# Attention seam and expert bias: joins, x with bias and part of the projection moved into the last unit, second bias as two rows

## The chip, the cores and the metric

One NeuronCore of a Trainium2 chip runs the kernel. The metric is the device time of one execution in microseconds (us), from runs of which the median is taken. TensorE (PE) multiplies, ScalarE (ACT), VectorE (DVE) and GpSimd (POOL) work element by element, SyncE (SP) issues nearly all DMAs. Each engine executes its instructions in order and is tied to the others by semaphores.

## What is computed

Three residual layers on x (8 x 64 tokens, 512 features), with a context of 8 x 1601 x 512:

```python
x = x + xattn(layernorm(x), ctx)      # 16 heads of 32 over 1601 keys: softmax(q k) v, then @ Wproj + bproj
x = x + attn(layernorm(x))            # 16 heads of 64, triu mask, only the diagonal of the softmax is used
x = x + moe(layernorm(x))             # 8 experts, each token goes to 2
# moe:  h = gelu(x @ W1[e] + b1[e]);  eo = h @ W2[e] + b2[e];  sum over e of gate[e] * eo
```

All is float32. Each operand of a large product is split in a high part (rounded to fp32r) and a low part (the rest), and a product is three matmuls: hi x hi, hi x lo, lo x hi.

## The kernel before

**Units.** Cross attention runs in 16 units, one for each batch element b and each of two chunks of the context (chunk 0: 7 tiles of 128 keys, chunk 1: 6). A unit has nine steps i = 0 to 8 over eight pairs of heads. In step i, TensorE turns the probabilities of pair i-1 (L816), computes scores for a later pair (L805), builds keys and values of the next chunk, and multiplies the turned probabilities with V (`outputs(i)`, L828). ScalarE casts the turned probabilities to PT (`probs_hi`, L505), and takes the exp of the next pair (L518). VectorE takes the maxima (L631), the low halves of PT (L640, L644) and the sum U of the two halves of the outputs (L676). PT has one buffer, so outputs(i), the turns of the next pair, `probs_hi` and the low halves form a loop. The last unit (BE, 1) has no keys and values left to make. Functions named `..._beside(i)` and `..._begin`, `..._between` put other work in its steps, on each engine at a fixed place.

**The seam.** The heads' outputs of batch elements 0 to 6 lie in DRAM (`o_heads`), each a sum over two chunks that must be weighted with factors. SP loads them as oA and the factors, spread over partitions, as oR (8 DMAs, L976). GpSimd adds the halves (L989), multiplies by oR (L1024) and joins the two chunks (L1027, `o_joined`). ScalarE and VectorE split the result in oT_hi (L1041) and oT_lo (L1104). Batch element 7 goes by another way: its U is moved by a product with sel7 (`new_outputs`, L1221), its factors are factor7 (four linked small operations on VectorE, L1130 to L1133), X7 (L1144) and a product with spread7 (L1252). `project` (L1210 to L1212) multiplies token tile t by Wproj, for contraction blocks m. VectorE adds the products to x_sum (`first_sum`, L1158), which holds x + bproj (L1162). `norm_vector` and `norm_scalar` normalise the sum, first for tiles 0 to 2, then for tile 3; TensorE turns it (L1265, L1271), ScalarE and VectorE split it in x2T_hi and x2T_lo (L1189, L1192), and the next layer's Q columns begin (L155). W2_hi and W2_lo are the parts of that layer's weights (L943 on ScalarE, L1018 and L1291 on GpSimd). `keep_busy` (L166) issues matmuls whose result is not used.

**The experts.** Weights come as 8 units of 1 MB for each expert through a ring of four (L1684), cast by ScalarE (L1851) and split by VectorE (L2034). Tokens are sorted by expert in DRAM into tiles of 128, ten in this run. For a tile TensorE makes hidden layer and output; the bias b1 enters as a product of ones with two rows, high and low part, in a tile of 128 partitions whose other rows are zero (L2146). b2 was loaded for each expert over all 128 partitions (L1696) and added by VectorE to the output (L2061).

SP's order around the change: old outputs, chunk factors out (L963), head weights 0 (L937), oR, bvc, Wp_raw, x_sum, bproj, head weights 1. GpSimd's order: halves, masks, W2_lo, joins.

## Time and profile before

| | us |
|---|---|
| median of 3 runs | 1383.21 (1383.02 to 1383.8) |
| the profiled execution | 1381.99 |
| its span, first to last instruction | 1380.2 |
| TensorE busy | 1335.9 (97%) |
| VectorE busy | 932.7 (68%) |
| ScalarE busy | 763.7 (55%) |
| GpSimd busy | 107.5 (8%) |
| mean granted TensorE clock | 0.997 of full |

A row of the timeline gives start and length in us, the engine, the line of the kernel, the operation and its tiles (output <- inputs), the count, and in brackets the idle time of the engine before it and what ended that. A row with a count above one merges neighbours, and its length runs to the end of the last. The chain is the work that ended last, followed back from the end: time on it is time of the kernel. The windows give each engine's busy time in a stretch.

### The profile page before, as it was taken

What the parts mean: (1) busy time and instruction counts of PE and PEld (TensorE: products, weight loads), DVE (VectorE), ACT (ScalarE), POOL (GpSimd) and SP (SyncE); (2) the same over time, 40 slices, a digit from 0 to 9 for tenths busy, and PEclk for the clock granted to TensorE, in tenths of its full rate; (3) what the DMA queues carried; (4) which work ended last, traced back from release to release, by engine and by line L of the source; (5) the groups of instructions that cost most, each with busy time, mean ns of one, the idle gap of its engine ahead of it and who ended that gap; (6) DMA issues with size and microseconds to landing.
All of it is one profiled execution on the core that took longest, in us unless ns stands there. A gap on an engine that the chain in (4) does not pass through costs nothing.

```text
span 1380.2 us, 22335 instructions
## 1 busy us (share of the span) xinstructions
PE 1335.9 (97%) x7573; PEld 1163.0 (84%) x7574; DVE 932.7 (68%) x1506; ACT 763.7 (55%) x1334; POOL 107.5 (8%) x85
## 2 busy tenths in 40 slices
PE   9999999999999999999999999988899989999998
PEld 7898988898889898888988989977688778888886
DVE  5566666667567666666666766658588956388885
ACT  6465555566456555555555655555331636478872
POOL 2000000000000000000000000035444130000002
PEclk9999999999999999999999999999999999999999
DMA  5211111110201112101111111274527566399993
GB/s 198 96 54 32 30 45 52 27 46 24 56 15 53 30 34 61 30 27 46 46 34 33 36 30 34 48 137 116 92 62 288 209 227 200 129 350 346 354 368 113
DMA packets 126854, 145.13 MB, mean 105 GB/s; under 512 B 64073, under 2 KB 67529, under 8 KB 126801
## 3 DMA queue, kind: packets, MB, share of 16 engines
q1 hardware_dynamic: 125536, 140.44, 32.9%
q0 software_dynamic: 1280, 4.20, 0.9%
q8 instruction: 23, 0.38, 0.1%
q14 instruction: 15, 0.11, 0.0%
HBM read 124.75 MB, written 19.86 MB: 105 GB/s over the span
## 4 chain that ended last, share of the span: by engine, by line
PE 77%; DVE 12%; issue 5%; ACT 3%; DMA 2%; SPq 1%; DVEq 0%; POOL 0%; ACTq 0%
PE ps_scores L155 13%; PE ps_scores L157 13%; PE ps_scores L156 13%; PE ps_out L828 6%; PE ps_turn L816 5%; PE ps_scores L805 5%; PE ps_out L2172 2%; PE ps_out L2174 2%; PE ps_out L2173 2%; PE ps_turn L706 2%; PE ps_scores L2151 2%; PE ps_scores L2149 2%; PE ps_scores L2150 2%; DVE stat L631 2%; DVE Ks L556 1%
## 5 line engine op out<-in xcount | busy, mean ns | idle before, releaser
L556 DVE SCALAR_TENSOR_TENSOR Ks<-ps_scores,bkc,Ks 64x384 fp32r<-64x384 f32 (+2 forms) x254 | 160.5, 632 | 143.3 <-ACT Ks L430 140.8
L155 PE MATMUL ps_scores<-cT_hi,Wkv_hi 128*128 128x384 f32 (+2 forms) x504 | 182.0, 361 | 0.0
L518 ACT ACTIVATE Pr<-ps_scores,stat 128x705 f32<-128x705 f32 (+1 forms) x128 | 119.5, 934 | 109.9 <-DVE stat L631 109.9
L157 PE MATMUL ps_scores<-cT_hi,Wkv_lo 128*128 128x384 f32 (+2 forms) x504 | 173.0, 343 | 0.0
L156 PE MATMUL ps_scores<-cT_lo,Wkv_hi 128*128 128x384 f32 (+2 forms) x504 | 172.5, 342 | 0.0
L562 DVE TENSOR_TENSOR Vs<-ps_scores,Vs 128x512 fp32r<-128x512 f32 (+1 forms) x103 | 71.2, 691 | 147.9 <-ACT Vs L434 147.2
L430 ACT ACTIVATE Ks<-ps_scores,bkc 64x384 fp32r<-64x384 f32 (+2 forms) x254 | 149.4, 588 | 39.1 <-PE ps_scores L157 35.5
L155 PE MATMUL ps_scores<-Wkv_hi,cT_hi 128*128 128x512 f32 (+1 forms) x412 | 170.0, 413 | 0.0
L505 ACT CAST PT<-ps_turn 128x512 fp32r<-128x512 f32 (+2 forms) x256 | 110.2, 483 | 102.1 <-PE ps_turn L816 101.3
L157 PE MATMUL ps_scores<-Wkv_hi,cT_lo 128*128 128x512 f32 (+1 forms) x412 | 161.8, 393 | 0.0
L156 PE MATMUL ps_scores<-Wkv_lo,cT_hi 128*128 128x512 f32 (+1 forms) x412 | 161.1, 391 | 0.0
L2034 DVE TENSOR_TENSOR wu_lo<-wu_raw,wu_hi 128x2048 fp32r<-128x2048 f32 x56 | 126.7, 2287 | 21.1 <-ACT wu_hi L1851 21.1
L640 DVE TENSOR_TENSOR PT<-ps_turn,PT 128x512 fp32r<-128x512 f32 (+2 forms) x256 | 130.0, 549 | 11.0 <-ACT PT L505 10.0
L828 PE MATMUL ps_out<-PT,Vs 128*128 128x256 f32 x832 | 123.1, 286 | 13.9 <-DVE PT L644 9.6
L434 ACT CAST Vs<-ps_scores 128x512 fp32r<-128x512 f32 (+1 forms) x103 | 60.4, 586 | 133.8 <-PE ps_scores L157 133.0
L828 PEld LDWEIGHTS ps_out<-PT,Vs 128*128 128x128 f32 x832 | 113.3, 189 | 24.6 <-DVE PT L644 12.7
L631 DVE TENSOR_REDUCE stat<-ps_scores 128x1 f32<-128x705 f32 (+1 forms) x128 | 125.7, 983 | 3.5 <-DVE stats L682 3.4
L816 PE MATMUL ps_turn<-ident,Pr 128*128 128x128 f32 x832 | 112.2, 273 | 0.0
L1851 ACT CAST wu_hi<-wu_raw 128x2048 fp32r<-128x2048 f32 x56 | 105.3, 1917 | 4.9 <-DMA wu_raw<-in_L_ffn_W_dram 4.6
L816 PEld LDWEIGHTS ps_turn<-ident,Pr 128*128 128x128 f32 x832 | 98.2, 141 | 5.7
L157 PEld LDWEIGHTS ps_scores<-cT_hi,Wkv_lo 128*128 128x128 f32 x504 | 94.8, 188 | 5.2
L156 PEld LDWEIGHTS ps_scores<-cT_lo,Wkv_hi 128*128 128x128 f32 x504 | 95.2, 189 | 4.0
(391 smaller groups left out, 2500.0 us busy)
## 6 DMA issues: line engine op xcount, KB each, us to landing
wu_raw<-in_L_ffn_W_dram SPq DMA_DIRECT2D x64, 1024.0 KB, 7.2
raw<-in_ctx_dram SPq DMA_DIRECT2D x16, 768.0 KB, 4.6
raw<-in_ctx_dram SPq DMA_DIRECT2D x8, 1024.0 KB, 5.2
raw<-in_ctx_dram SPq DMA_DIRECT2D x8, 512.0 KB
sorted_x<-zeros SPq DMA_DIRECT2D x1, 4096.0 KB, 15.3
sorted_out<-zeros SPq DMA_DIRECT2D x1, 4096.0 KB, 25.6
o_heads<-U SPq DMA_DIRECT2D x56, 64.0 KB, 1.7
oA<-o_heads SPq DMA_DIRECT2D x8, 448.0 KB, 9.1
```

Source lines behind the costliest of these rows:

```text
L155: nc.tensor.matmul(out_ap, sh, mh, start=(i == 0), stop=False)
L156: nc.tensor.matmul(out_ap, sh, ml, start=False, stop=False)
L157: last = nc.tensor.matmul(out_ap, sl, mh, start=False, stop=(i == len(pairs) - 1))
L430: ins = nc.scalar.activation(Ks[c][0:64, 2 * i + h, o:o + wide], acc[64 * h:64 * h + 64, 0:wide], ACT.Identity, bias=bkc[:, 2 * i + h:2 * ...
L505: ins = nc.scalar.copy(PT[:, full[0]:full[-1] + 1, 0, :], acc[:, 0:P * len(full)].rearrange("p (t r) -> p t r", r=P))
L518: nc.scalar.activation(Pr[:, i % 2, 0:VALID[c]], S_cols(c, 0, VALID[c], 0 if ctx else i % 2), ACT.Exp, bias=stat[:, 0, c, i:i + 1], accum_ ...
L556: ins = nc.vector.scalar_tensor_tensor(out=Ks[c][64:128, j, o:o + wide], in0=acc[64 * h:64 * h + 64, 0:wide], scalar=bkc[:, j:j + 1], in1= ...
L631: nc.vector.tensor_reduce(stat[:, 0, c, i:i + 1], S_cols(c, 0, VALID[c], 0 if ctx else i % 2), AX.X, ALU.max, negate=True).then_inc(sem("s ...
L640: ins = nc.vector.tensor_tensor(PT[:, full[0]:full[-1] + 1, 1, :], acc[:, 0:P * len(full)].rearrange("p (t r) -> p t r", r=P), f32(PT[:, f ...
L816: ins = nc.tensor.matmul(bank(P_BANKS[q])[0:M, at:at + P], Pr[:, (i - 1) % 2, t * P:t * P + M], ident[:, :], is_transpose=True, start=True ...
L828: ins = nc.tensor.matmul(psO_heads, Vs[c][0:M, t, i - 1, :], PT[0:M, t, :, :].rearrange("p a r -> p (a r)"), start=(t == 0), stop=(t == CH ...
L2034: nc.vector.tensor_tensor(wu_lo[v][:, :, :], wu_raw[v % RING][:, :, :], f32(wu_hi[v][:, :, :]), ALU.subtract).then_inc(sem("wu_lo_done"), 1)
```

## The change

In the last unit and the seam: oR is loaded as soon as the last chunk-0 scores are made, then Wproj and bproj, before the head weights; x_sum comes after Wp_lo, whose raw input shares its place. The joins stand ahead of three of the masks and of W2_lo on GpSimd, which also adds bproj to x. Wp_hi is cast by ScalarE at the end of the unit before, Wp_lo follows in step 0, oT_hi in steps 2 to 5, oT_lo in steps 3 to 6, W2_hi[0] in two halves in steps 6 and 7. Token tile 0 and a block of tile 1 are projected inside the unit, with fewer `keep_busy`. The second layer's normalised x is written by ScalarE for tiles 0 to 2, with a shift, as the third layer's is. In the experts: b2 is split in high and low part with b1, written to DRAM, loaded as two rows for each expert, and added by a product of ones in TensorE's last part of the output; VectorE copies where it added. Some tiles move in SBUF.

```diff
-            sp.wait_ge(sem("kv_made"), KV_LAST + PIECES[1])
-            load_head_weights(sp, 0)
-            sp.wait_ge(sem("o_summed"), PAIRS_0 + NP + 1)
+            sp.wait_ge(sem("s_made"), PAIRS_0 + NP)
             sp.wait_ge(sem("r_out"), 32)
             for c in range(2):
                 for jj in range(2):
                         r0 = 64 * jj + HD * h
                         src = r_dram[c, h].rearrange("(m jj) t -> jj m t", jj=2)[jj][:, 0:OLD]
                         sp.dma_start(oR[r0:r0 + HD, c, :, :], src.partition_broadcast(HD)).then_inc(sem("oR_in"), 16)
+            sp.dma_start(Wp_raw[:, :, :], Wproj.rearrange("(k p) n -> p k n", p=P)).then_inc(sem("wp_in"), 16)
+            sp.wait_ge(sem("oA_in0"), 64)
+            sp.dma_start(bpr[:, :], bproj.partition_broadcast(P)).then_inc(sem("x_again"), 16)
+            sp.wait_ge(sem("kv_made"), KV_LAST + PIECES[1])
             sp.dma_start(bvc[:, :], bkv[D:2 * D].rearrange("(m p) -> p m", p=P),
                          allow_slow_non_contiguous=True).then_inc(sem("bv_in"), 16)
-            sp.dma_start(Wp_raw[:, :, :], Wproj.rearrange("(k p) n -> p k n", p=P)).then_inc(sem("wp_in"), 16)
+            load_head_weights(sp, 0)
+            sp.wait_ge(sem("wp_lo"), 1)
             sp.dma_start(x_sum[:, :, :], x_rows).then_inc(sem("x_again"), 16)
-            sp.wait_ge(sem("oA_in0"), 64)
-            sp.dma_start(bpr[:, :], bproj.partition_broadcast(P)).then_inc(sem("x_again"), 16)
             load_head_weights(sp, 1)
...
+            pool.wait_ge(sem("o_added"), 2 * KC)
+            pool.wait_ge(sem("oR_in"), 128)
+            for m in range(KC):
+                join(m)
+            nc.gpsimd.memset(triu[:, :, :], 1.0).then_inc(sem("masks_set"), 1)
+            nc.gpsimd.memset(diag[:, :], 0.0).then_inc(sem("masks_set"), 1)
+            nc.gpsimd.memset(spread7[:, :, :], 0.0).then_inc(sem("masks_set"), 1)
+            pool.wait_ge(sem("masks_set"), 4)
...
+            pool.wait_ge(sem("x_again"), 32)
+            for t in range(TT):
+                ins = nc.gpsimd.tensor_tensor(x_sum[:, t, :], x_sum[:, t, :], bpr[:, :], ALU.add)
+            ins.then_inc(sem("x_base"), 1)
             pool.wait_ge(sem("sw_hi"), 1)
-            nc.gpsimd.tensor_tensor(W2_lo[0][:, :, :], W2_raw[0][:, :, :], f32(W2_hi[0][:, :, :]), ALU.subtract) \
-                .then_inc(sem("sw_lo"), 1)
-            pool.wait_ge(sem("oR_in"), 128)
-            for m in range(KC):
-                pool.wait_ge(sem("o_added"), KC + m + 1)
-                for c in range(2):
-                    nc.gpsimd.tensor_tensor(oA[c][:, 0, m, :], oA[c][:, 0, m, :], oR[:, c, m, :], ALU.mult) \
-                        .then_inc(sem("o_scaled"), 1)
-                pool.wait_ge(sem("o_scaled"), 2 * m + 2)
-                nc.gpsimd.tensor_tensor(oA[0][:, 0, m, :], oA[0][:, 0, m, :], oA[1][:, 0, m, :], ALU.add) \
-                    .then_inc(sem("o_joined"), 1)
+            for k in range(KC):
+                ins = nc.gpsimd.tensor_tensor(W2_lo[0][:, k, :], W2_raw[0][:, k, :], f32(W2_hi[0][:, k, :]), ALU.subtract)
+            ins.then_inc(sem("sw_lo"), 1)
...
+            elif i == 8:
+                act.wait_ge(sem("wp_in"), 16)
+                act.wait_ge(sem("o_made"), PAIRS_0 + NP)
+                nc.scalar.copy(Wp_hi[:, :, :], Wp_raw[:, :, :]).then_inc(sem("wp_hi"), 1)
 
         def scalar_old_hi(act, m):
             act.wait_ge(sem("bv_in"), 16)
             if i == 0:
                 act.wait_ge(sem("o7_turned"), 1)
                 nc.scalar.copy(o7[:, 0, 0, :, :], o7_bank(0)).then_inc(sem("o7_in"), 1)
-            elif i == 1:
-                head_weights_hi(act, 0)
-            elif 4 <= i < NP:
-                if i == 5:
-                    act.wait_ge(sem("wp_in"), 16)
-                    nc.scalar.copy(Wp_hi[:, :, :], Wp_raw[:, :, :]).then_inc(sem("wp_hi"), 1)
-                elif i == 7:
-                    act.wait_ge(sem("shifted7"), 1)
-                    nc.scalar.activation(part7[:, :, :], part7[:, :, :], ACT.Exp).then_inc(sem("exp7"), 1)
-                scalar_old_hi(act, i - 4)
+            elif 2 <= i < 2 + KC:
+                scalar_old_hi(act, i - 2)
+            elif i == 6:
+                act.wait_ge(sem("sw_in0"), 64)
+                nc.scalar.copy(W2_hi[0][:, 0:2, :], W2_raw[0][:, 0:2, :])
+            elif i == 7:
+                act.wait_ge(sem("shifted7"), 1)
+                nc.scalar.activation(part7[:, :, :], part7[:, :, :], ACT.Exp).then_inc(sem("exp7"), 1)
+                nc.scalar.copy(W2_hi[0][:, 2:KC, :], W2_raw[0][:, 2:KC, :]).then_inc(sem("sw_hi"), 1)
...
+            act.wait_ge(sem("ln_scaled"), 2)
+            for t in FIRST_TILES:
+                ins = nc.scalar.activation(xn2[:, t, :], x_sum[:, t, :], ACT.Identity,
+                                           bias=shift2[:, t:t + 1], scale=lnt2[4][:, t:t + 1])
+            ins.then_inc(sem("x_base"), 1)
+            norm_scalar(act, 3, lnt2, LAST_TILE)
             turned_hi(0)
             turned_hi(1)
-            norm_scalar(act, 3, lnt2, LAST_TILE)
...
-            if i == 5:
-                vector_old_lo(dve, 0)
-            elif i == 6:
+            if i == 0:
+                dve.wait_ge(sem("wp_hi"), 1)
+                nc.vector.tensor_tensor(Wp_lo[:, :, :], Wp_raw[:, :, :], f32(Wp_hi[:, :, :]), ALU.subtract) \
+                    .then_inc(sem("wp_lo"), 1)
+            elif 3 <= i < 3 + KC:
+                vector_old_lo(dve, i - 3)
...
-                dve.wait_ge(sem("wp_hi"), 1)
-                nc.vector.tensor_tensor(Wp_lo[:, :, :], Wp_raw[:, :, :], f32(Wp_hi[:, :, :]), ALU.subtract) \
-                    .then_inc(sem("wp_lo"), 1)
-            elif i == 7:
-                vector_old_lo(dve, 1)
...
-            dve.wait_ge(sem("x_again"), 32)
-            nc.vector.tensor_tensor(x_sum[:, :, :], x_sum[:, :, :],
-                                    bpr[:, :].unsqueeze(1).broadcast_to([P, TT, D]), ALU.add) \
-                .then_inc(sem("x_base"), 1)
-            vector_old_lo(dve, 2)
-            vector_old_lo(dve, 3)
...
-            norm_vector(dve, 2, x_sum, xn2, lnt2, FIRST_TILES, prepare=summed)
+            norm_vector(dve, 2, x_sum, xn2, lnt2, FIRST_TILES, prepare=summed, shift=shift2)
...
-            elif i in (2, 3):
+            elif i == 5:
                 pe.wait_ge(sem("o7_in"), 1)
-                keep_busy(3, 6)
-            elif 4 <= i < 7:
-                keep_busy(1, 6)
+                pe.wait_ge(sem("wp_lo"), 1)
+                project(pe, 0, (0,))
+            elif i == 6:
+                project(pe, 0, (1,))
             elif i == 7:
-                keep_busy(1, 6)
                 pe.wait_ge(sem("o_summed"), PAIRS_1 + NP - 1)
                 new_outputs(pe, 1, slice(0, KC - 1))
-                keep_busy(6, 6)
             elif i == 8:
-                pe.wait_ge(sem("o7_in"), 1)
-                pe.wait_ge(sem("wp_lo"), 1)
-                for t in FIRST_TILES:
-                    project(pe, t, (0,))
+                project(pe, 0, (2, 3))
+                project(pe, 1, (0,))
...
-            for t in FIRST_TILES:
-                project(pe, t, range(1, KC))
+            project(pe, 1, range(1, KC))
+            project(pe, 2, range(KC))
...
-            pe.wait_ge(sem("ln_done"), 2)
+            pe.wait_ge(sem("x_base"), 2)
...
-            keep_busy(8, SPREAD_BANK)
-            pe.wait_ge(sem("ln_done"), 3)
+            keep_busy(3, SPREAD_BANK)
+            pe.wait_ge(sem("ln_done"), 2)
...
-                sp.dma_start(b2row[:, :], b2[bass.ds(e, 1), :].rearrange("a d -> (a d)").partition_broadcast(P)) \
-                    .then_inc(sem("b2row_in"), 16)
+                sp.dma_start(f32(b2rows[0:2, :]), b2_dram[:, bass.ds(e * D, D)]).then_inc(sem("b2row_in"), 16)
...
-            sp.dma_start(b1_raw[:, :], b1.rearrange("e (c p) -> (e c) p", p=P)).then_inc(sem("b1_in"), 16)
+            sp.dma_start(b_raw[:, 0:P], b1.rearrange("e (c p) -> (e c) p", p=P)).then_inc(sem("b1_in"), 16)
+            sp.dma_start(b_raw[:, P:P + B2], b2.rearrange("e (c p) -> (e c) p", p=B2)).then_inc(sem("b1_in"), 16)
...
+            for part, half in enumerate((b_hi, b_lo)):
+                sp.dma_start(b1_dram[part].rearrange("(r c) -> r c", c=P), f32(half[:, 0:P])) \
+                    .then_inc(sem("b1_out"), 16)
+                sp.dma_start(b2_dram[part].rearrange("(r c) -> r c", c=B2), f32(half[:, P:P + B2])) \
                     .then_inc(sem("b1_out"), 16)
             load_next(0, 5)
-            sp.wait_ge(sem("b1_out"), 32)
+            sp.wait_ge(sem("b1_out"), 64)
...
+            pool.wait_ge(sem("x_sorted"), 16 * 2 * TT)
+            pool.wait_ge(sem("g_turned"), 1)
+            nc.gpsimd.memset(f32(b2rows[:, :]), 0.0).then_inc(sem("b1rows_zeroed"), 1)
...
-                dve.wait_ge(sem("b2row_in"), 16 * (e + 1))
                 dve.wait_ge(sem("eo_stored"), t * 16 + EO_CREDIT)
-                nc.vector.tensor_tensor(eo[:, :], bank(7), b2row[:, :], ALU.add) \
+                nc.vector.tensor_copy(eo[:, :], bank(7)) \
...
+                    if q == QT - 1:
+                        pe.wait_ge(sem("b2row_in"), 16 * (e + 1))
+                        nc.tensor.matmul(bank(7), ones_r[:, :], b2rows[:, :], start=False, stop=False)
```

## Rows read from the trace of the kernel before

**Rows 1.** The page, section 4: the chain that ended last, by engine.
```profile
PE 77%; DVE 12%; issue 5%; ACT 3%; DMA 2%; SPq 1%; DVEq 0%; POOL 0%; ACTq 0%
```

**Rows 2.** Waits of ScalarE, 905 to 985 us: total us, times, longest.
```profile
ACT oT_hi L1041 <- POOL oA L1027: 4.8, 3, 3.0
```

**Rows 3.** Timeline of SP: start and length of issue, line, target, count.
```profile
903.79 1.26 SPq L963 DMA_DIRECT2D chunk_factors<-factorT  x2
...
919.77 2.95 SPq L937 DMA_DIRECT2D sW_raw<-in_L_attn_WQ_dram  x4
922.81 5.51 SPq L976 DMA_DIRECT2D oR<-chunk_factors  x8
```

**Rows 4.** Landing (us after issue), rate in 40 slices of 919 to 950, chain.
```profile
chunk_factors<-factorT SPq DMA_DIRECT2D x2, 32.0 KB, 5.7
...
GB/s 0 0 63 243 274 223 215 233 238 217 189 204 227 194 220 215 194 222 213 167 174 354 367 396 381 388 383 386 319 252 228 77 227 193 228 37 0 21 0 0
...
927.89 9.10 DMA oR<-chunk_factors
```

**Rows 5.** Timeline of the last unit (start, us): ScalarE exp and Wp_hi, TensorE.
```profile
922.24 0.85 ACT L518 ACTIVATE Pr<-ps_scores,stat 128x705 f32<-128x705 f32 x1 [1.88 <-DVE stat L631]
922.57 1.96 PE L1221 MATMUL ps_turn<-U,sel 128*128 128x256 f32 x8 [0.46 <-issue]
926.81 0.95 PE L828 MATMUL ps_out<-PT,Vs 128*128 128x256 f32 x6 [0.98 <-issue]
...
932.26 1.43 PE L828 MATMUL ps_out<-PT,Vs 128*128 128x256 f32 x6 [2.53 <-DVE PT L644]
...
936.54 0.96 PE L828 MATMUL ps_out<-PT,Vs 128*128 128x256 f32 x6
...
939.73 0.99 PE L828 MATMUL ps_out<-PT,Vs 128*128 128x256 f32 x6 [0.71 <-DVE PT L644]
...
942.82 1.91 ACT L1053 CAST Wp_hi<-Wp_raw 128x2048 fp32r<-128x2048 f32 x1
...
946.94 0.98 PE L828 MATMUL ps_out<-PT,Vs 128*128 128x256 f32 x6 [1.48 <-DVE PT L644]
...
957.18 0.98 PE L828 MATMUL ps_out<-PT,Vs 128*128 128x256 f32 x6 [0.23 <-DVE PT L644]
```

**Rows 6.** Timeline of VectorE and GpSimd where both read SBUF.
```profile
930.75 4.53 POOL L1018 TENSOR_TENSOR sW_lo<-sW_raw,sW_hi 128x2048 fp32r<-128x2048 f32 x1 [6.94 <-ACT sW_hi L943]
...
948.30 0.58 DVE L1113 TENSOR_TENSOR top<-stat 128x8 f32<-128x8 f32 x1
...
948.92 1.07 DVE L1116 TENSOR_TENSOR part<-top,stat 128x16 f32<-128x16 f32 x1
...
949.91 2.28 DVE L1119 TENSOR_TENSOR Wp_lo<-Wp_raw,Wp_hi 128x2048 fp32r<-128x2048 f32 x1
```

**Rows 7.** Windows: busy us of each engine (PE first), PEclk, DMA share, GB/s.
```profile
932.00:936.00 4.00, 3.74 (x17) 3.74 (x18) 2.23 (x6) 1.67 (x6) 3.28 (x1) 0.57 1.10 224
...
978.00:982.00 4.00, 2.20 (x8) 1.69 (x8) 4.00 (x6) 2.76 (x3) 0.95 (x1) 0.79 0.94 146
```

**Rows 8.** Timeline of the seam: the third sum, the link, first Q matmul.
```profile
967.28 0.69 DVE L1158 TENSOR_TENSOR x_sum<-x_sum,ps_scores 128x512 f32<-128x512 f32 x1 [0.18 <-PE ps_scores L1212]
...
974.18 2.43 DVE L132 TENSOR_TENSOR rs<-rt 128x1 f32<-128x1 f32 x1
...
980.27 0.77 PE L155 MATMUL ps_turn<-x2T_hi,sW_hi 128*128 128x512 f32 x1 [1.80 <-DVE x2T_lo L1192]
```

**Rows 9.** Timeline of the same chain in front of the experts.
```profile
1090.54 0.69 DVE L1895 TENSOR_TENSOR x_sum<-x_sum,ps_scores 128x512 f32<-128x512 f32 x1 [0.69 <-PE ps_scores L1539]
...
1099.62 0.68 DVE L1922 TENSOR_TENSOR x3T_lo<-ps_scores,x3T_hi 128x512 fp32r<-128x512 f32 x1
```

**Rows 10.** Experts, lines view (busy us, mean ns); a window as in rows 7.
```profile
L2146 PE MATMUL ps_scores<-b1rows,ones_r 128*128 128x512 f32 x36 | 15.0, 416 | 0.0
...
1240.00:1300.00 60.00, 59.11 (x275) 47.94 (x274) 50.90 (x34) 49.12 (x42) 0.00 (x0) 1.00 1.00 349
```

66 lines of the change are left out of this document (37 added, 29 removed).

## Prediction, made before the change was run

> **What bounds the kernel now.** The page's chain comes first: TensorE carries 77% of it [rows 1], so a stall counts only where it stops TensorE or ends last. The change touches four stretches: the last attention unit (920 to 958 us), the seam behind it (to 980 us), the start of the experts (1080 to 1126 us) and the expert loop (to 1370 us).
>
> In the last unit the waits show ScalarE held 4.8 us by GpSimd's joins of the old heads' outputs [rows 2]. The joins start late because their factors oR were issued at 922.81 us, behind the head weights, and landed at 936.99 us (927.89 + 9.10) [rows 3, 4]. The reader is to see the rhythm of the `outputs` matmuls in [rows 5]: the natural step is 3.19 us (936.54 to 939.73), but outputs 1 to 6 took 20.13 us instead of 16.0, and 6 to 8 took 10.24 us. In the seam, the first Q matmul waits for VectorE: from the third `first_sum` (967.28) to 980.27 us are 12.99 us, of which one 128x1 operation took 2.43 us [rows 8]. The experts' loop is TensorE's: even where transfers are at share 1.00 it is busy 59.11 of 60 us [rows 10].
>
> **Part 1, loads.** oR now waits only for unit 7's last chunk-0 scores (about 909 us) and r_out. r_out's first store starts at 903.79 [rows 3] and the pair needs 5.7 us to land [rows 4]; the second started 0.65 us after the first, so oR starts at 910.2 us. Of the eight, 229,376 bytes each, 1.84 MB at the about 210 GB/s that such rows move [rows 4] take 8.75 us. The first bytes move 1.3 us after an issue (sW_raw issued 919.77 [rows 3], rate row up at about 921), and a landing shows 2.0 us after the last byte (2.88 MB of weights and oR from 921.3 would end at 935.0, the landing is at 936.99). So oR lands at 910.2 + 1.3 + 8.75 + 2.0 = 922.3 us, 14.7 us earlier. Wp_raw, 1.05 MB at 385 GB/s [rows 4], follows 2.7 us later: 925.0 us. The weights of head unit 0, now behind both, are wanted at step 6 only; x_sum waits for Wp_lo and lands at about 936 us, before GpSimd asks for it.
>
> **Part 2, the start of the last unit: a new wait.** ScalarE's cast Wp_hi (1.91 us [rows 5]) stands before the exp of pair 0, and waits for Wp_raw. Queued behind it is that exp, which began at 922.24 us [rows 5], and behind the exp TensorE's turns, so all of the unit. The exp now starts at 925.0 + 1.9 = 926.9. From exp to outputs 1 were 4.57 us (922.24 to 926.81), of which 0.9 was TensorE finishing the new outputs (922.57 + 1.96 = 924.53 [rows 5]) after the exp was ready; so 926.9 + 3.7 = 930.6. VectorE's Wp_lo (2.28 us) now stands before the low halves of pair 1 and can meet a GpSimd join; I add 0.4 of a possible 1.1. Outputs 1: **931.0 us, 4.2 later** than 926.81.
>
> **Part 3, the rest of the unit.** The joins run from 922.3 to about 938 us (3 operations of 1.14 us each, four times, plus up to 2.28 for Wp_lo), each done before its ScalarE step; the joins' waits are gone. W2_hi leaves step 1 and goes in halves (0.96 us) into steps 6 and 7, where the 3.19 us step has 1.1 us of ScalarE free. The two projections in steps 5 and 6, 3 matmuls of 0.23 us each, fit under TensorE's wait. Steps 1 to 6 would take 5 x 3.19 = 16.0 us. Two costs come on top. The clock: before, step 2 to 3 took 4.28 us while the granted clock fell to 0.57 [rows 5, 7], 1.1 us over natural. Now TensorE idles longer, from 923.6 to 928 us, and the filler matmuls are gone; I take the same 1.1. And oT_lo, which reads two SBUF tiles, meets GpSimd's new x additions: up to one of them (about 1.1 us) at each meeting, as `top` and `part` in [rows 6]; with oT_lo VectorE's step is nearly full, so this shows: 0.7 in all, bounds 0 and 2.2. Outputs 6: 931.0 + 17.8 = 948.8 us (before 946.94).
>
> Steps 6 to 8 took 10.24 us. Wp_lo (2.28) and one oT_lo (0.68) leave VectorE's path: 7.3. But GpSimd's W2_lo moves from step 2 to behind ScalarE's cast in step 7: 4 operations of about 1.2 us (a quarter of 4.53 [rows 6], and the start of each), running from 0.6 to 5.5 us after outputs 7. VectorE starts factor7 1.45 us after outputs 7; three of its four links read two SBUF tiles. [rows 6] show such links of 128x8 and 128x16 elements taking 0.58 and 1.07 us instead of about 0.17: each waits for the GpSimd operation that runs, the next one then slips in. So each of the three ends with a GpSimd operation, at 2.0, 3.4 and 4.8 us, instead of the last at 2.25: +2.5 us. Outputs 8: 948.8 + 7.3 + 2.5 = **958.6 us, 1.4 later** than 957.18.
>
> The Trainium skill, SBUF — State Buffer, Who interferes with whom, says that a VectorE instruction with two SBUF inputs contends with a GpSimd instruction that reads SBUF, and, under SBUF: two separate sides, that the one that starts first has the pair for the whole instruction. The trace [rows 6] agrees with the lock. By the rule alone VectorE may also win the gaps and lose one operation only: the sum would be lower by 1.5 to 2.5 us, rival B below.
>
> **Part 4, the seam.** Off VectorE go x + bias (2.28) and two oT_lo (1.27), but behind them it waited for the copy of o7 in any case, so only some 0.8 us of start is won. TensorE's projection shrinks by 6 matmuls, and the third sum, no longer held by it, starts 9.1 us after outputs 8 instead of 10.1 (957.18 to 967.28): 1.0 won. From there the new order is one the kernel already has in front of the experts: third sum 1090.54, last low half at 1099.62 + 0.68 = 1100.30: 9.76 us [rows 9], against 12.99. That includes ScalarE's three normalisations (2.22 us for VectorE's 1.46), and it does without the 2.43 us link, which stood behind a GpSimd operation that is now released only after the last tile. 3.2 won. Together **-4.2 us**. Nothing new is late: the K weights' low part is done some 9 us before use.
>
> The clock at the first Q matmuls is 0.79 over 978 to 982 us already [rows 7]; TensorE now idles 3.4 us before the turns where it idled 1.2, with 3 fillers for 8. Turns at the lower level would cost 0.4; I take **+0.4** (bounds -1.6, the eight slow matmuls gone, and +1.5).
>
> **Part 5, experts.** One more matmul for each of 10 tiles: like the b1 product, 36 of these lie at 0.236 us spacing on TensorE (0.416 in their overlapped record [rows 10]). In the last tile it hides under VectorE's fetched sums; 9 x 0.236 = 2.1 us. Each b2 load falls from 256 KB to 4 KB, 0.7 us of transfer at 349 GB/s. Where that can be felt, 1240 to 1300 us, TensorE lacks 0.9 us in all [rows 10]; I take 0.6 back. **+1.5 us** (bounds 0 and +2.2). The wait for the row moves from VectorE to TensorE, behind which the next tile queues; the row is issued with the previous tile's result and wanted 20 us later, with a longest landing of 8.0 us for the larger form. At the start SP issues three more small DMAs (b2 in, two parts out, some 0.4 us each), which delay unit 5's weights by about 1 us against 10 us of slack; the wider casts add 0.1 us under up's matmuls; the memset of b2rows delays its load by 0.6 us with 4 to spare: 0. The copy that replaces the add in the last tile is worth -0.1 to 0.
>
> **Sum**: 1.4 - 4.2 + 0.4 + 1.5 = -0.9 us. The profiled execution took 1381.99 us around its span of 1380.2; the median of the runs is 1383.21. The difference is applied to the median: **1382.3 us**. About 2.8 us (0.2%) is what a measurement of this kernel tells from no change.
>
> **The rivals.**
> A, the forecast: gain in the seam, given back by Wp_hi's wait, by the lock in step 7 and by the matmuls. 0.50; own range 1380.5 to 1385.5.
> B, no collision in step 7: W2_lo loses the gaps to VectorE, or starts late enough. -2.5 more: 1379.8 us. For it: the rows show only two links in a row, and the lock could go to VectorE between GpSimd's operations. Against: both of these lost that gap. 0.25, and mostly beyond the 0.2%.
> C, slower: without fillers the clock stays low through the unit. Each of the five steps then costs 1.1 us as step 2 to 3 did, +4.4 more: 1386.7 us. It decides from the first step on at which TensorE's work no longer lifts the clock; for it: that idle of 4.4 us; against: in the low level TensorE was busy 3.74 of 4 us and the clock rose again [rows 7]. The Trainium skill, TensorE: Matmul & The Clock Gate, What's actually happening, has the throttled state as the default that activity releases, which speaks against fewer fillers. 0.13.
> D, the b2 product is free: TensorE's matmul fills the loop's waits and the lighter loads give back the rest, -1.5: 1380.8 us; with an earlier Wp_raw (by 1 us) 1379.8. 0.12.
>
> **How the numbers follow.** Faster takes 0.22 of B, 0.06 of A and 0.06 of D: 0.34. Slower takes the 0.12 of C and 0.04 of A: 0.16. The rest, 0.50, is within 0.2%. The range takes A's and D's and most of B and goes up to near C: 1379.0 to 1386.2.
>
> **What would show it.** Right: oR landed by 923 us; a ScalarE gap before Wp_hi ending near 925; outputs 1 near 931; links of factor7 of about 1 us; seam of about 19 us from outputs 8 to Q; tiles longer by 0.24 us. Wrong: Wp_raw there by 922 (3 us better), factor7 links of 0.2 us, a granted clock below 1.00 beyond 936 us, or a TensorE wait for b2rows.

## The result, and the profile after

The changed kernel takes **1379.18 us** (median of 17 runs, 1377.41 to 1382.37) beside 1383.21 us of the kernel before in the same session: ratio 0.9974, 95% interval 0.9967 to 0.9981, so 3.6 us faster by the ratio, between 2.6 and 4.6. The profiled execution took 1380.16 us around a span of 1377.4; it lies 1.0 above its median, and that of the kernel before 1.2 below its own, so the two traces show less of the gain than the medians do.

The page after: span, engines' busy time, and the chain that ended last.

```profile
span 1377.4 us, 22276 instructions
PE 1333.5 (97%) x7541; PEld 1158.8 (84%) x7542; DVE 930.1 (68%) x1503; ACT 766.4 (56%) x1338; POOL 114.1 (8%) x93
...
PE 80%; DVE 11%; issue 4%; ACT 3%; DMA 2%; SPq 0%; DVEq 0%; ACTq 0%
```

TensorE's share of the chain rose from 77% [rows 1] to 80%: waits went away, its work did not. Where they went is read from six marks, each the start of the same instruction in both traces:

| mark, us | before | after | difference |
|---|---|---|---|
| outputs 1 of the last unit | 926.81 | 929.70 | +2.9 |
| outputs 8 | 957.18 | 956.31 | -0.9 |
| third sum of the seam | 967.28 | 966.97 | -0.3 |
| first Q matmul | 980.27 | 978.22 | -2.1 |
| third sum ahead of the experts | 1090.54 | 1086.95 | -3.6 |
| last `eo` | 1372.02 | 1369.01 | -3.0 |

The loads and the start of the last unit (timelines of SP, GpSimd, ScalarE and TensorE; start, length, engine, line).

```profile
910.38 3.64 SPq L975 DMA_DIRECT2D oR<-chunk_factors  x8
914.06 0.43 SPq L976 DMA_DIRECT2D Wp_raw<-in_L_xattn_Wproj_dram  x1
...
921.93 2.22 POOL L995 TENSOR_TENSOR oA<-oA,oR 128x448 f32<-128x448 f32 x2
...
924.00 1.90 ACT L1050 CAST Wp_hi<-Wp_raw 128x2048 fp32r<-128x2048 f32 x1 [3.79 <-DMA Wp_raw<-in_L_xattn_Wproj_dram]
925.81 0.84 ACT L519 ACTIVATE Pr<-ps_scores,stat 128x705 f32<-128x705 f32 x1
...
929.70 1.62 PE L829 MATMUL ps_out<-PT,Vs 128*128 128x256 f32 x6 [1.38 <-issue]
```

oR is issued 12.4 us earlier than in [rows 3], and the joins run. But ScalarE now waits 3.79 us for the projection weights behind oR, and the exp of pair 0, 922.24 us in [rows 5], starts at 925.81. That is the new wait.

The step from outputs 7 to outputs 8: VectorE's four links of factor7 beside GpSimd's W2_lo.

```profile
950.40 0.98 PE L829 MATMUL ps_out<-PT,Vs 128*128 128x256 f32 x6 [0.30 <-DVE PT L645]
...
951.35 4.98 POOL L1037 TENSOR_TENSOR sW_lo<-sW_raw,sW_hi 128x512 fp32r<-128x512 f32 x4 [6.19 <-ACT sW_hi L1070]
...
951.76 0.91 DVE L1147 TENSOR_TENSOR factor<-part,stat 128x16 f32<-128x16 f32 x1
952.70 1.20 DVE L1148 TENSOR_TENSOR top<-factor 128x8 f32<-128x8 f32 x1
953.94 0.20 DVE L1149 RECIPROCAL top<-top 128x8 f32<-128x8 f32 x1
954.18 0.96 DVE L1150 TENSOR_TENSOR factor<-part,top 128x16 f32<-128x16 f32 x1
...
956.31 1.52 PE L829 MATMUL ps_out<-PT,Vs 128*128 128x256 f32 x6 [2.22 <-DVE PT L645]
957.63 3.01 PE L1261 MATMUL ps_scores<-X,spread 128*128 128x512 f32 x4
```

Three links of 128 x 8 or 128 x 16 elements take about 1 us each. The reciprocal, which reads one tile, takes 0.20. The step takes 5.91 us. Meanwhile TensorE idles 2.22 us, and the six matmuls of outputs 8 then take 1.52 us where those of outputs 7 took 0.98.

That is the clock. The windows view after (busy us of PE, PEld, DVE, ACT, POOL with counts, then granted clock, DMA share, GB/s):

```profile
930.00:934.00 4.00, 3.34 (x17) 3.04 (x16) 1.99 (x6) 1.79 (x6) 3.92 (x4) 0.68 0.95 303
954.00:958.00 4.00, 1.78 (x8) 1.65 (x8) 3.55 (x8) 0.00 (x0) 2.33 (x2) 0.81 0.00 0
958.00:962.00 4.00, 4.00 (x15) 2.29 (x14) 0.37 (x2) 0.37 (x1) 0.37 (x1) 0.76 0.00 0
974.00:978.00 4.00, 2.82 (x14) 2.41 (x12) 2.64 (x6) 2.19 (x5) 3.67 (x1) 0.63 1.39 218
978.00:982.00 4.00, 3.78 (x16) 3.10 (x17) 3.03 (x2) 2.44 (x2) 3.50 (x2) 1.00 0.63 99
1240.00:1300.00 60.00, 59.99 (x282) 48.75 (x281) 50.84 (x33) 48.43 (x43) 0.00 (x0) 1.00 0.97 345
```

The granted clock is below full three times: at the unit's start (as before, [rows 7]), behind the links, and at the turns of the seam. At the first Q matmuls, 978 to 982 us, it is 1.00, where it was 0.79 in [rows 7].

The seam and the experts: VectorE's third sum, ScalarE's normalisation (which took VectorE's place), the first Q matmul, the third sum ahead of the experts, and, from the lines view, the new product and the copy that replaced the addition.

```profile
966.97 0.67 DVE L1175 TENSOR_TENSOR x_sum<-x_sum,ps_scores 128x512 f32<-128x512 f32 x1
...
970.39 2.22 ACT L1086 ACTIVATE xn<-x_sum,shift,rs 128x512 f32<-128x512 f32 x3 [1.23 <-DVE shift L138]
...
978.22 0.50 PE L155 MATMUL ps_turn<-x2T_hi,sW_hi 128*128 128x512 f32 x1 [1.40 <-DVE x2T_lo L1203]
...
1086.95 0.69 DVE L1912 TENSOR_TENSOR x_sum<-x_sum,ps_scores 128x512 f32<-128x512 f32 x1 [0.50 <-PE ps_scores L1549]
...
L2077 DVE COPY eo<-ps_out 128x512 f32<-128x512 f32 x10 | 6.8, 684 | 3.7 <-PE ps_out L2193 3.7
L2186 PE MATMUL ps_out<-b2rows,ones_r 128*128 128x512 f32 x10 | 4.7, 472 | 0.0
```

From the third sum to Q are 11.25 us, where [rows 8] give 12.99. The expert loop is full in this trace: 59.99 of 60 us, 59.11 in [rows 10].

### The profile page after: what moved, and what is told of

Its sections match the earlier page's. It is cut to its first block, busy times and chain, and to the rows that moved or that the text cites. A ratio compares the mean times of both kernels' runs of the same rounds, so it can differ in the third digit from the quotient of the medians.

```text
span 1377.4 us, 22276 instructions
## 1 busy us (share of the span) xinstructions
PE 1333.5 (97%) x7541; PEld 1158.8 (84%) x7542; DVE 930.1 (68%) x1503; ACT 766.4 (56%) x1338; POOL 114.1 (8%) x93
## 4 chain that ended last, share of the span: by engine, by line
PE 80%; DVE 11%; issue 4%; ACT 3%; DMA 2%; SPq 0%; DVEq 0%; ACTq 0%
PE ps_scores L155 13%; PE ps_scores L157 12%; PE ps_scores L156 12%; PE ps_out L829 6%; PE ps_turn L817 5%; PE ps_scores L806 5%; PE ps_scores L2167 3%; PE ps_scores L2165 3%; PE ps_scores L2166 3%; PE ps_out L2191 3%; PE ps_out L2193 3%; PE ps_out L2192 3%; PE ps_turn L707 2%; DVE stat L632 2%; DVE PT L641 1%
```

## The experiments

The theory of the forecast: what the seam wins is given back at three places, by Wp_hi's wait (some 3 us at outputs 1), by the lock between VectorE and GpSimd in step 7 (2.4 us), and by TensorE's extra matmuls. Rivals: the links are slow for another reason; what is won in the unit doesn't reach the end; or something not in the sum, the clock above all, decides. All ratios are to the kernel before, run in the same session; e1 to e4, e5 to e8 and e9 to e12 are one session each, and no run of the changed kernel but e9 stands in them, so times are compared with it through these ratios.

### The two waits taken away, one by one and together

W2_lo behind step 7, by a wait for X7, which VectorE makes after the links:

```diff
             pool.wait_ge(sem("sw_hi"), 1)
+            pool.wait_ge(sem("x7"), 2)
             for k in range(KC):
                 ins = nc.gpsimd.tensor_tensor(W2_lo[0][:, k, :], ...
```

> The changed kernel, with GpSimd's W2_lo[0] held back until X7 is made (one more wait ahead of it). Theory (lock, then clock): VectorE's links of factor7 take 0.17 us again instead of 0.91, 1.20 and 0.96; outputs 8 start 3.6 us after outputs 7 instead of 5.91 (2.3 won); TensorE's idle of 2.2 us before outputs 8 is gone, so the granted clock does not fall behind it and spread7 takes 1.9 us instead of 3.0, another 1.1 to 1.5 won: the first Q matmul 3.4 to 3.8 us earlier, the time 3.5 us below the changed kernel. Rival 1 (the lock only moves): W2_lo now meets the additions of o7, two of which read SBUF twice; they take up to 1.3 us each longer, so only 0 to 2 us are won. Rival 2 (clock on its own): the clock falls in the seam all the same; 2.3 us.

Ratio 0.9969 (0.9957 to 0.9981), 1379.03 us. VectorE's links and the operations behind them, and GpSimd's W2_lo:

```profile
952.02 0.17 DVE L1149 TENSOR_TENSOR top<-factor 128x8 f32<-128x8 f32 x1
952.23 0.20 DVE L1150 RECIPROCAL top<-top 128x8 f32<-128x8 f32 x1
952.46 0.18 DVE L1151 TENSOR_TENSOR factor<-part,top 128x16 f32<-128x16 f32 x1
...
958.61 2.35 DVE L1183 SCALAR_TENSOR_TENSOR o<-o,bvc 128x64 f32<-128x64 f32 x4
...
955.49 5.00 POOL L1038 TENSOR_TENSOR sW_lo<-sW_raw,sW_hi 128x512 fp32r<-128x512 f32 x4 [10.26 <-DVE X L1162]
```

Without GpSimd the links take 0.17 to 0.20 us and the step 3.53 us in place of 5.91: GpSimd's operations beside them are the cause. The granted clock, which fell behind the links in after, is 1.00 over 954 to 962 here. But W2_lo now meets four small additions of step 8, which take 2.35 us for 0.87 in after, and the third sum is 2.6 us earlier (964.42) and not 3.5. So are Q (975.63) and the experts' third sum (1084.36); at the last `eo` 1.6 us are left (1367.39). That last microsecond is no effect of the edit that a trace could show: from the experts' third sum to the last `eo` this run takes 283.03 us and after 282.06, but after run again takes 282.92. The ratio is only 0.7 us better than after's, and the two intervals overlap almost wholly. So the lock's cost in its step is shown; that removing it in this way shortens the kernel is not.

The projection weights first:

```diff
             sp.wait_ge(sem("s_made"), PAIRS_0 + NP)
+            sp.dma_start(Wp_raw[:, :, :], ...).then_inc(sem("wp_in"), 16)
             sp.wait_ge(sem("r_out"), 32)
             ...                                   # the eight oR loads
-            sp.dma_start(Wp_raw[:, :, :], ...).then_inc(sem("wp_in"), 16)
```

> The changed kernel, with the load of Wproj issued ahead of the oR loads, before the wait for r_out. Theory (the new wait of ScalarE is worth what it delays): Wp_raw lands near 915.5 us, Wp_hi starts when unit 15's outputs are made (about 920.4), exp of pair 0 at 922.4 instead of 925.8, outputs 1 near 926.9 instead of 929.7 (2.8 won); TensorE's idle of 2.9 us goes and with it the clock's fall over 929 to 932 (another 1.0): outputs 6 some 3.8 us earlier. The joins start 2.7 us later but still before their ScalarE steps. Time 2.8 to 3.8 us below the changed kernel. Rival (the joins become the bound): oT_hi waits for GpSimd, and what is won at outputs 1 is lost by outputs 6: 0 to 1 us.

Ratio 0.9948 (0.9933 to 0.9964), 1375.57 us, some 3.6 below after. ScalarE's cast and the exp, and the granted clock of the unit's start:

```profile
920.76 1.90 ACT L1050 CAST Wp_hi<-Wp_raw 128x2048 fp32r<-128x2048 f32 x1 [0.31 <-PE ps_out L829]
922.57 0.84 ACT L519 ACTIVATE Pr<-ps_scores,stat 128x705 f32<-128x705 f32 x1
...
926.00:930.00 4.00, 2.65 (x19) 2.38 (x20) 3.07 (x8) 2.52 (x8) 3.92 (x5) 1.00 0.91 167
930.00:934.00 4.00, 3.07 (x25) 2.78 (x25) 2.81 (x7) 2.47 (x7) 3.92 (x4) 1.00 1.12 332
```

The weights are there before ScalarE asks. Outputs 1 stands at 926.43. TensorE's longest pause before outputs 1 is 0.97 us where it was 2.88, and the clock stays full: steps 1 to 2 take 3.19 us where they took 4.26. The third sum is 4.4 us earlier (962.55), Q 5.9 (972.35); 1.5 of these lie between the two marks, where the turns ran at the full clock in this execution, far behind the edit. One new cost shows: GpSimd's x additions, now at 941.93 to 947.3, meet the links `top` and `part` of step 6 (1.23 and 1.19 us), and outputs 6 to 7 take 5.55 us in place of 3.37. In step 7 the first link is through in 0.17 us although W2_lo is being made, and the two others take 1.19 and 0.97: a link pays for up to one of them, and not always.

Both edits together, with nothing else changed:

> Both of the edits of the two runs before in one kernel. Theory: the two costs lie one after the other on TensorE's path, so they add: 6 to 7 us below the changed kernel, some 10 us below the kernel before. Rival (they share a cause, the clock or VectorE's load): less than 5 us below the changed kernel.

Ratio 0.9950 (0.9937 to 0.9963), 1377.14 us. The two do not add. With the weights first, the clock had just fallen behind the slow step 6 (0.93 over 946 to 950, 0.65 over 950 to 954), and in step 7 TensorE's projection matmuls, 0.43 us apart, filled the time that the free links offered: outputs 8 at 953.37, 953.51 without it. At the third sum the two kernels are level (962.41 and 962.55). Behind it this execution loses 3.3 us more: TensorE waited 2.7 us for h_lo, the low half of the hidden layer, in the expert loop (1.3 in the other), and the granted clock was 0.80 and 0.77 over 1104 to 1112, where it was 1.00. Neither stretch holds anything that the two edits change.

### Each part of the change alone

The experts' part on the kernel before:

```diff
-                sp.dma_start(b2row[:, :], b2[bass.ds(e, 1), :]....partition_broadcast(P)) ...
+                sp.dma_start(f32(b2rows[0:2, :]), b2_dram[:, bass.ds(e * D, D)])....
...
-                dve.wait_ge(sem("b2row_in"), 16 * (e + 1))
-                nc.vector.tensor_tensor(eo[:, :], bank(7), b2row[:, :], ALU.add) \
+                nc.vector.tensor_copy(eo[:, :], bank(7)) \
...
+                        pe.wait_ge(sem("b2row_in"), 16 * (e + 1))
+                        nc.tensor.matmul(bank(7), ones_r[:, :], b2rows[:, :], start=False, stop=False)
```

> The kernel before, with the experts' part of the change alone (b2 in two rows, product of ones, copy). Theory from the marks of the two traces: 9 matmuls of 0.236 us, less the stalls of 0.9 us that the lighter loads remove, and 0.3 us in the start: 0.6 to 1.0 us slower than the kernel before. Rival 1: only the matmuls count, 2.1 us slower. Rival 2: hidden, 0 within 0.5 us.

Ratio 1.0009 (1.0000 to 1.0017). From the experts' third sum to the last `eo` the trace shows 283.04 us; before 281.48, after 282.06. Taken from these traces the part costs 0.6 to 1.6 us, and by this ratio 1.2, between 0 and 2.4. The stretch varies by itself, though: over the ten traces with the new form it is 281.93 to 283.36 us and once 286.76, with the old one 280.09, 281.48 and two that hold a stall told below. In the later part of the loop, where TensorE waits for nothing, one `eo` follows the other after 25.73 us with the product (after) and after 25.50 us without it (the first trace of the seam alone, below): these 0.23 us are the product's own price.

The attention part with the experts as before, that is, after with the diff just shown turned round:

> The attention and seam part of the change alone; the experts keep the bias copied out by eight bias rows and the addition. If the two parts are independent: the third sum of the normalisation before the experts 3.6 us earlier than before (at 1087.0 as in after), nothing lost in the expert loop, so the time is 3.6 to 4.8 us below before (0.9965 to 0.9974), and 0 to 1.2 us below after. Rival: the expert part paid only in company with the seam (its loads out of the way of the seam's): then this run gains clearly less than after, 2 us or less below before.

Ratio 0.9996 (0.9986 to 1.0005), 1382.25 us. Its profiled execution, 1376.19, was the shortest of twelve and shows the marks of after, or better ones (third sum 967.50, Q 977.29, experts' third sum 1086.02, last `eo` 1366.11). So the trace speaks for the first theory and the median for the rival. Both kernels, unchanged, were run again side by side:

> The changed kernel once more, beside the others of this call. The two parts of the change, timed apart, came to +1.2 us (experts) and -0.9 (seam), the whole to -4.0 in another call. If these two parts really help one another: again 3.5 to 4.5 us below before, and clearly below the seam part alone. If the sum was a matter of which call and chip they ran in: 0 to 1.5 us below before here. The trace should again show outputs of step 8 at 956 to 957, and a low granted clock in 926 to 934 and 954 to 962; whether it is low in 970 to 982 is the open point.

Ratio 0.9962 (0.9949 to 0.9976), 1380.18 us. The trace repeats after's marks: outputs 8 at 956.59, Q at 978.39, experts' third sum at 1087.13. The gain is there again, 5.3 us by the ratio and 4.8 by the medians, where 3.5 to 4.5 were expected if the parts help one another.

> The seam part alone once more. Its median was 1382.25, but its profiled execution, at 1376.19, was the shortest of its twelve, and had the full clock from 962 on. If the rest of its executions are longer through a low clock at the turns or the first Q matmuls, this second trace shows it: granted clock of 0.5 to 0.8 somewhere in 970 to 986, first Q matmul at 978 to 981. If the seam is as in the first trace and the time is lost among the experts, the last expert addition less the third sum before the experts is 282 us or more (280.1 in the first trace, 282.1 in after, 281.5 in before).

Ratio 0.9978 (0.9966 to 0.9989), 1382.73 us. The experts' part, alone a cost, is worth 2 to 3 us beside this seam in both pairs of runs; in this second pair, the only one run side by side, the intervals overlap. The profiled execution, 1388.44, was the longest of its twelve, as the first had been the shortest. The second trace shows both things of which either was expected: clock 0.66 and 0.50 over 974 to 982 with Q at 979.00, and 289.4 us from the experts' third sum to the last `eo`, with a stall that no term of the sum had (the rest are two longer tiles earlier, in which TensorE waited 3.0 us for h_lo, and a granted clock of 0.59 behind the stall). Another part of it is at the start of the unit: the projection weights landed at 925.73, 1.7 us later than in after, and outputs 1 stands at 931.48. The first matmul of the last tile, in this run and in another one with the old form of the experts (e12, below):

```profile
1350.84 0.76 PE L2156 MATMUL ps_scores<-b1rows,ones_r 128*128 128x512 f32 x1 [3.46 <-issue]
...
1340.10 0.47 PE L2160 MATMUL ps_scores<-b1rows,ones_r 128*128 128x512 f32 x1 [3.66 <-issue]
```

"Issue" means that nothing in the profile released it. In the second, from 1337.8 us to the matmul the 16 DMA engines moved nothing but a few packets of a store in the last slice, so it waited for no weights:

```profile
DMA  0000000000000000000000000000000000000006
...
q1 hardware_dynamic: 7, 0.01, 1.6%
```

In both traces a packet of the instruction queue q8 moved 0.4 to 1.4 us after TensorE had fallen idle (within 0.5 us from 1337.32 and from 1347.74), and TensorE began more than 2 us after it. In all ten traces with the new form it moved 0.2 to 1.2 us before the tile's start, with no stall. Before and the first trace of the seam alone had it within 0.5 us of that start, the latter behind it, and no stall; so the packet's place alone doesn't decide. The last expert's tile is code of its own behind the loop. So: two of four traces with the old form stall 3.5 us, none of ten with the new one. That it is TensorE's instructions coming late is argued from these times, not shown by a run that changes nothing else. The Trainium skill, Runtime: NRT & Kernel Launch, Instruction fetch mechanics, says that a branch to code outside the two pages held makes the engine wait for a DMA fetch; the place and the packet agree.

### The normalisation, and the clock in front of it

The second layer's normalised rows back to VectorE:

```diff
-            act.wait_ge(sem("ln_scaled"), 2)
-            for t in FIRST_TILES:
-                ins = nc.scalar.activation(xn2[:, t, :], x_sum[:, t, :], ACT.Identity, ...)
-            ins.then_inc(sem("x_base"), 1)
-            norm_scalar(act, 3, lnt2, LAST_TILE)
             turned_hi(0)
             turned_hi(1)
+            norm_scalar(act, 3, lnt2, LAST_TILE)
...
-            norm_vector(dve, 2, x_sum, xn2, lnt2, FIRST_TILES, prepare=summed, shift=shift2)
+            norm_vector(dve, 2, x_sum, xn2, lnt2, FIRST_TILES, prepare=summed)
```

> After, but the normalised rows of the second layer go back from ScalarE to VectorE, with the old order of waits. Forecast: from the third sum to the first Q matmul the old 12.8 to 13.0 us in place of 11.25, so Q 1.6 us later than after, and the time 1.2 to 2.0 us above after. Rival: the move cost nothing or was worth nothing (TensorE would have turned at the low clock either way): less than 0.5 us from after.

Ratio 1.0007 (0.9997 to 1.0017), more than 4 us above after; 1.2 to 2.0 were forecast. The link and the first Q matmuls:

```profile
974.03 2.42 DVE L132 TENSOR_TENSOR rs<-rt 128x1 f32<-128x1 f32 x1
...
980.18 0.79 PE L155 MATMUL ps_turn<-x2T_hi,sW_hi 128*128 128x512 f32 x1 [1.40 <-DVE x2T_lo L1198]
980.77 0.63 PE L156 MATMUL ps_turn<-x2T_lo,sW_hi 128*128 128x512 f32 x1
```

The 2.43 us link of [rows 8] is back, Q stands 13.02 us behind the third sum as before, and the first Q matmuls run at the lower level, 0.43 us apart for 0.23. The experts' third sum is at 1090.81, 3.9 us later than after and where it was before (1090.54). So at that mark this one edit takes back the whole gain: 2.0 us at Q, and as much again in matmuls that ran at the low clock. The forecast for this run left the second half out.

The first half is the edit's. The second is the edit's only in part, as the fourteen traces show side by side (us; two kernels were traced twice):

| traces | third sum to Q | Q to experts' third sum |
|---|---|---|
| old order of the normalisation: before, e4, e6 | 12.99 to 13.05 | 110.27 to 110.63 |
| new order, full clock from 966 us on: e2, e3, e5, e8 | 9.79 to 9.80 | 108.72 to 108.73 |
| new order, dummies in the gap: e11 (below) | 10.82 | 108.75 |
| new order, low clock at the turns: after, e1, e9, e12 | 11.11 to 11.37 | 108.73 to 108.74 |
| new order, low clock at Q: e7, e10 | 10.80 and 12.05 | 110.06 and 110.13 |

With the old order the first Q matmuls ran at the low clock in three traces of three, with the new one in two of eleven, one of which (e10) is of the same kernel as one with the full clock (e5). So with the new order that loss of 1.3 to 1.9 us was seen less often, and it is not excluded.

The gap in front of the turns filled with dummies:

```diff
-            keep_busy(4, SPREAD_BANK)
+            keep_busy(22, SPREAD_BANK)
             pe.wait_ge(sem("x_base"), 2)
```

> After, with 22 dummy matmuls in place of 4 before the turns of the second layer's x, where TensorE had 2.71 us of idle time; each took 0.13 us. If that idle time is what drops the granted clock (0.94 and 0.63 in 970 to 978 in after, and 0.6 or less in two other kernels with its seam): clock 0.9 or more in 970 to 982, turns spaced as at full clock, first Q matmul 1.0 to 1.5 us earlier relative to the third sum (9.8 to 10.3 us in place of 11.25), and the time 1 to 2 us below after. Rival: the turns wait for the rows and not for TensorE, or the dummies run past the rows' arrival: less than 0.3 us.

Ratio 0.9957 (0.9944 to 0.9970); 1379.63 us beside 1380.18 for after in the same session. The windows, the dummies and the turns:

```profile
970.00:974.00 4.00, 4.00 (x39) 4.00 (x38) 3.00 (x13) 2.32 (x4) 0.00 (x0) 1.00 1.12 214
974.00:978.00 4.00, 2.60 (x25) 2.36 (x23) 3.17 (x7) 3.02 (x6) 3.48 (x1) 1.00 0.96 196
...
969.09 5.07 PE L166 MATMUL ps_scores<-ident 128*128 128x128 f32 x44
973.99 1.15 PE L1274 MATMUL ps_turn<-ident,xn 128*128 128x128 f32 x9
```

The clock stays full, and from the turns to Q pass 3.99 us where after needs 5.55 (972.67 to 978.22): the low clock costs 1.6 us there. But the dummies, 44 records for 22, overrun: the turns start 6.83 us behind the third sum where after's start 5.70 behind it, so 1.1 of the 1.6 us are lost again and Q is only 0.4 us nearer to the third sum (10.82 us). The clock did what the theory says; the dose was too large, and the 1 to 2 us expected are not seen in the time. One trace can't exclude that the clock would have stayed full without the dummies, as it did in e5.

### Smaller pieces for GpSimd

W2_lo in 16 operations of 128 columns in place of 4 of 512:

```diff
             for k in range(KC):
-                ins = nc.gpsimd.tensor_tensor(W2_lo[0][:, k, :], ...
+                for c in range(4):
+                    cc = slice(c * P, (c + 1) * P)
+                    ins = nc.gpsimd.tensor_tensor(W2_lo[0][:, k, cc], ...
```

> After, with W2_lo of the first Q weights made in 16 pieces of 128 columns in place of 4 of 512, in the same place, beside step 7. If each small VectorE link of step 7 waits for the GpSimd operation that is running (pieces of 1.25 us: links of 0.91, 1.20 and 0.96), links of at most 0.4 us each, outputs of step 8 at 954.2 to 954.9 in place of 956.31, and no collision moved on to the additions of step 8. The time then 0.5 to 2 us below after. Rival: the links are slow whenever GpSimd runs at all, whatever the size of its operations: links stay at 0.9 us or more, or there are more of them, and the time is after's.

Ratio 0.9964 (0.9951 to 0.9977). VectorE's links beside GpSimd's pieces:

```profile
954.82 0.17 DVE L1149 TENSOR_TENSOR factor<-part,stat 128x16 f32<-128x16 f32 x1
955.02 0.32 DVE L1150 TENSOR_TENSOR top<-factor 128x8 f32<-128x8 f32 x1
955.37 0.20 DVE L1151 RECIPROCAL top<-top 128x8 f32<-128x8 f32 x1
955.61 0.17 DVE L1152 TENSOR_TENSOR factor<-part,top 128x16 f32<-128x16 f32 x1
...
954.41 7.63 POOL L1039 TENSOR_TENSOR sW_lo<-sW_raw,sW_hi 128x128 fp32r<-128x128 f32 x16 [9.06 <-ACT sW_hi L1072]
```

A link now waits for at most one short piece: 0.17 to 0.32 us, and the step takes 3.56 us with GpSimd running all through it. The price is 7.63 us of GpSimd for 4.98, which nobody waited for. Nothing clear of this is seen in the time: the ratio is that of after, 0.9974 and 0.9962, within its interval. In this execution outputs 7 came at 953.46 for 950.40. The projection weights had landed 1.1 us later (925.06), outputs 1 was 1.6 us later, and 1.4 more were lost in the steps behind it: the granted clock was low over 926 to 938 (0.58, 0.50, 0.64), and an oT_lo beside GpSimd's x additions took 1.69 us for 0.68. The clock was low again over 970 to 982, and Q came at 978.22 as in after. Outputs 8 at 954.2 to 954.9 was missed for these reasons: it came at 957.02.

Weights first, and both GpSimd jobs in such pieces:

> Projection weights loaded first (as in the run with that alone, 3.6 us below after) and both GpSimd jobs of steps 6 and 7 (x with bias, and W2_lo) in 16 pieces of 128 columns in place of 4 of 512. In that run step 6 to 7 took 5.5 us with links of 1.23 and 1.19 beside the x additions, and 7 to 8 took 5.2. If the piece's length sets a link's wait: step 6 to 7 3.5 to 3.9 us, step 7 to 8 3.8 to 4.3, outputs of step 8 at 950.6 to 951.6 in place of 953.51, the third sum 1.5 to 2.5 us earlier than 962.55, and the time 1 to 2.5 us below that run, 1373.0 to 1374.5. Rival: the chain of the seam is then bound by TensorE's matmuls of the projection that fill those steps (6 at half clock, 0.43 us each), or the pieces' own fixed cost lengthens the GpSimd job into step 8: less than 0.5 us gained.

Ratio **0.9941** (0.9928 to 0.9955), 1374.37 us: the best time of the study, 8 us below before by the ratio. Step 6 to 7 takes 3.96 us, 7 to 8 3.89, outputs 8 stands at 950.65, the third sum at 960.31 and the first Q matmul at 970.10, 10 us earlier than before. The windows:

```profile
946.00:950.00 4.00, 3.24 (x20) 2.95 (x21) 2.79 (x9) 1.95 (x5) 4.00 (x11) 1.00 0.00 0
950.00:954.00 4.00, 3.81 (x22) 2.42 (x20) 2.43 (x6) 0.00 (x0) 4.00 (x8) 1.00 0.00 0
966.00:970.00 4.00, 2.64 (x22) 2.40 (x22) 3.75 (x12) 2.99 (x7) 2.33 (x1) 1.00 1.38 217
```

No window from 918 us to the last `eo` is below 0.98. With the same seam and the experts as before, so e8 with the experts' diff turned round:

> The best seam so far (projection weights loaded first, both GpSimd jobs in pieces of 128 columns) with the experts as they were before: bias rows copied out and added by VectorE. With the experts' part costing what the traces of it alone show (0.7 to 1.2 us): 1373.2 to 1373.8, 0.5 to 1.2 below 1374.37. Rival, that the experts' new form pays when the seam is tight, as the medians of after and of the seam alone read: 2 to 3 us above 1374.37.

Ratio 0.9932 (0.9916 to 0.9948), 1376.37 us. As a time that is the rival's 2 us above e8; but the kernel before took 1384.98 beside it and 1383.19 beside e8, and against it the two intervals overlap, although this trace has the 3.66 us stall. With this seam the runs don't tell the two forms of the experts apart. The turns of this trace ran at the low clock (0.57 over 966 to 970) and Q came at 971.89, although the seam is e8's.

## Why the prediction was right or wrong

The forecast time, 1382.3, was 3.1 us above the measured one, which lies just inside the whole range (1379.0) and outside A's own (1380.5 to 1385.5); "within 0.2%" had most of the chance and the kernel is 0.26% faster. By its number the result is nearest to B, whose mechanism, no collision in step 7, the runs refute. So the number fell into the range by luck in part. Of the signs given, oR, the ScalarE gap and the links came as said; the seam of about 19 us from outputs 8 to Q did not (21.9), and one sign of being wrong was there: a granted clock below 1.00 beyond 936 us (0.81 and 0.76 over 954 to 962, 0.63 over 974 to 978). Point by point:

- **Loads: right.** The joins start at 921.93 (oR 922.3 forecast), Wp_raw is there at 924.0 (925.0).
- **Outputs 1:** forecast +4.2, measured +2.9: 1.0 of the error is Wp_raw's landing, which itself differs between executions (924.00, 924.20, 925.06 and 925.73 in after, e9, e7 and e10). That this wait is real, and the largest single cost of the change that a run took away, e2 shows: 3.6 us.
- **The unit's steps:** 17.3 us from outputs 1 to 6 (17.8 forecast). The one low-clock step is there, 4.26 us, and no other, so rival C did not come. In e2, where TensorE doesn't wait long for the exp, even that one is gone.
- **The lock in step 7: right, and shown.** Three links of about 1 us, as A said and B denied; e1 and e7 take them away, each in its own way. The Trainium skill, SBUF — State Buffer, SBUF: two separate sides, has the first starter hold the shared ports for its whole instruction; e7 agrees, as the link's wait shrinks with the piece (1.20 to 0.32 us). It isn't one operation for every link, as I had it: in e2 one of the three took 0.17 us.
- **Seam, in front of Q: over-valued.** Forecast 9.1 + 9.76 us from outputs 8 to Q, measured 10.66 + 11.25. The misses are clock: behind the links outputs 8 takes 1.52 us for 0.98 and the products with spread7 3.01 us (windows 954 to 962), and in front of Q the turns run at 0.63 (974 to 978). In the borrowed chain of [rows 9] the clock was full, which I took over unasked. Where it was full in the new seam too, both terms came out as forecast: 9.79 us from the third sum to Q in four traces (9.76 forecast), 9.04 from outputs 8 to the third sum in e2 and e3 (9.1 forecast). So the chain was read rightly, and the term that was mis-sized is the clock's, put at 0.4: 1.5 us in front of Q in after (1.6 by e11) and 1.6 behind the links.
- **Seam, behind Q: mis-sized, with the wrong sign.** I took +0.4 for the clock at the first Q matmuls, with -1.6 as the far bound. It is -1.5: from Q to the experts' third sum 108.73 us, before 110.27. e6, where the low clock returns with the old order, has the loss again. In after the low level fell on the turns, which are few, and was over before Q; before, it fell on Q's first eight matmuls. In e7 and e10, with the same order, it fell on Q again (110.06 and 110.13 us), so part of this gain is luck of the profiled execution.
- **The experts:** forecast +1.5; the traces say +0.6 in company (282.06 less 281.48), +1.6 alone, and +1.8 between the shortest of each form (281.93 in e8, 280.09 in e5). The product costs what it was said to, 0.23 us a tile. That it or the lighter loads take the place of waits, the 0.6 us of the forecast, is not shown: over 1240 to 1300 us TensorE was busy 60.00 us in e5 with the old form, and 58.60 to 60.00 in the traces with the new one. What the sum did not know is the stall of 3.5 us in front of the last tile, which the old form has in some executions.

In sum, on the trace: outputs 8 came 2.3 us earlier than forecast, the way to Q took 3.0 more, the way behind Q 1.9 less and the experts 0.9 less. That is 2.1 us on the good side, and the span fell by 2.8 us instead of 0.9. The medians differ by 4.0; the last microsecond is no row's, but before's traced execution was a short one and after's a long one. The mechanism of A was right, its collision too. In this pair of traces the result is on the faster side of the forecast because outputs 8 came early and the low clock did not fall on Q.

Open: why the experts' part costs 1.2 us by itself, gives 2 to 3 us beside after's seam and nothing that the runs can tell beside e8's; the stall accounts for the sign only if it is frequent, and one or two traces a kernel can't say how frequent. Open too is what decides whether the clock falls at the turns and at Q.

## What to carry to other kernels

When a small chain on VectorE runs beside a GpSimd job that reads SBUF, count up to one GpSimd operation for every link that reads two tiles, and cut the GpSimd job in pieces rather than move it: moved, it meets the next chain; cut, it costs GpSimd time, which nobody waited for here. Read which matmuls run at the low granted clock, before and after: when a change moves them from a dense stretch to a thin one, that can be worth as much as the wait it removes (2 us each in e6). Take more than one trace before you count on it, because the same kernel shows it both ways. A load moved forward must be put in the order in which its users block others: here the smaller transfer behind the larger one held the whole unit.
